# A four-layer graph network on one core: bounds of row numbers kept in registers, and norms without small operations for mean, variance and epsilon

## What is computed

```python
def _layernorm(x, axis=-1, eps=1e-05):
    m = jnp.mean(x, axis=axis, keepdims=True)
    v = jnp.var(x, axis=axis, keepdims=True)
    return (x - m) / jnp.sqrt(v + eps)
...
h = jnp.maximum(_layernorm(x, axis=-1), 0.0)
x = x + _L0_gnn_ref(h, src, dst)                    # degree-normalised sum of neighbours
h = jnp.maximum(_layernorm(x, axis=-1), 0.0)
x = x + _L1_gnn_ref(h, edge_index, L1_gnn_theta)    # polynomial of the Laplacian, 4 steps
h = jnp.maximum(_layernorm(x, axis=-1), 0.0)
x = x + _L2_gnn_ref(h, ..., src, dst, edge_type_86) # relation weights, gate, self loop
h = jnp.maximum(_layernorm(x, axis=-1), 0.0)
x = x + _L3_gnn_ref(h, src, dst)                    # 10 steps, h = 0.9 * A h + 0.1 * h0
```

## Time and profile before

| what | before |
|---|---|
| runs | 2785.8, 2788.61 and 2793.77 us, median 2788.61 |
| profiled execution | 2789.32 us, span 2779.9 us |
| DVE busy | 1768.5 us, 64% |
| POOL busy | 1800.6 us, 65% |
| PE busy | 430.6 us, 15% |
| ACT busy | 335.7 us, 12% |
| HBM traffic | 77.00 MB, 28 GB/s on average |
| clock granted to PE | 1.0 |

### The profile page before, as it was taken

The page is one execution under the profiler, slowest core; times in us unless marked ns, Lnnn a source line. Parts: engine busy times, 40 slices in busy tenths (PEclk is TensorE's granted clock), DMA queues, the critical chain, the costliest instruction groups (busy, mean ns, idle before and its releaser), DMA issues.

```text
span 2779.9 us, 14498 instructions
## 1 busy us (share of the span) xinstructions
PE 430.6 (15%) x2105; PEld 214.1 (8%) x2105; DVE 1768.5 (64%) x3130; ACT 335.7 (12%) x1043; POOL 1800.6 (65%) x1786
## 2 busy tenths in 40 slices
PE   0000000000010000000000098294195000006000
PEld 0000000000010000000000033031131000006000
DVE  8998896666679967177766678587878921420000
ACT  0000021111100110011111144141042200000000
POOL 6666677777554471575777456766456777466776
DMA  1001022221100130110301100100000120000000
GB/s 20 15 11 26 15 61 50 50 50 31 28 9 6 62 127 22 33 57 20 101 25 18 18 3 4 11 2 6 5 7 8 62 63 10 29 11 7 11 8 8
DMA packets 68026, 77.00 MB, mean 28 GB/s; under 512 B 34799, under 2 KB 60872, under 8 KB 67192
## 3 DMA queue, kind: packets, MB, share of 16 engines
q0 software_dynamic: 56384, 23.45, 6.4%
q1 hardware_dynamic: 5720, 27.38, 2.5%
q10 hardware_dynamic: 5856, 25.60, 2.4%
HBM read 35.67 MB, written 46.87 MB: 30 GB/s over the span
## 4 chain that ended last, share of the span: by engine, by line
DVE 49%; issue 25%; POOL 9%; PE 7%; another core or an unknown queue 6%; DMA 2%; ACT 2%; DVEq 1%; POOLq 0%; ACTq 0%; SPq 0%
POOL out L1568 8%; DVE mf L520 7%; DVE pay L520 4%; DVE z L520 3%; DVE psum L915 3%; DVE outs L520 2%; DVE psum L523 2%; PE psum L2009 2%; DVE mf L902 2%; DVE xs L902 2%; DVE xs L897 2%; PE psum L2010 2%; DVE st L544 1%; DVE mf L897 1%
## 5 line engine op out<-in xcount | busy, mean ns | idle before, releaser
L1562 POOL DMA_INDIRECT xs<-in_x,i_src x196 | 200.0, 1020 | 131.2 <-issue 53.9
L1568 POOL DMA_INDIRECT out<-outs,i_outS x196 | 205.2, 1047 | 117.3 <-issue 60.8
L1562 POOL DMA_INDIRECT xd<-x_rows,i_dstX x196 | 204.6, 1044 | 112.5 <-DVE z L1374 66.7
L1562 POOL DMA_INDIRECT xd<-in_x,i_dst x196 | 205.2, 1047 | 111.2 <-DVE mf L520 42.6
L1562 POOL DMA_INDIRECT mf<-x_rows,i_srcX x196 | 200.5, 1023 | 94.5 <-issue 64.3
L1568 POOL DMA_INDIRECT out<-outs,i_srcX x196 | 196.3, 1001 | 71.5 <-issue 58.9
L1562 POOL DMA_INDIRECT pay<-payload_by_dst,i_rank x196 | 195.1, 996 | 62.6 <-issue 62.6
L520 DVE TENSOR_TENSOR mf<-mf 128x128 f32<-128x128 f32 (+5 forms) x578 | 175.1, 341 | 12.2 <-DVE mf L520 1.9
L520 DVE TENSOR_TENSOR pay<-psum,pay 128x512 f32<-128x512 f32 x196 | 132.5, 688 | 66.5 <-ACT pay L1887 56.2
L2009 PE MATMUL psum<-pay 64*128 64x512 f16 x196 | 117.4, 599 | 117.2 <-ACT pay L1872 77.3
L1932 PE MATMUL psum<-ident,small 128*128 128x128 f32 x4 | 1.6, 501 | 851.2 <-DVE small L960 851.2
(11 more groups left out here) (458 smaller groups left out, 2479.9 us busy)
## 6 DMA issues: line engine op xcount, KB each, us to landing
z<-in_x ACTq DMA_DIRECT2D x14, 624.0 KB
out<-z ACTq DMA_DIRECT2D x14, 624.0 KB
l_first_rows<-mf SPq DMA_DIRECT2D x2, 3234.0 KB, 9.7
outs<-in_x ACTq DMA_DIRECT2D x6, 624.0 KB
out<-outs ACTq DMA_DIRECT2D x6, 624.0 KB
l_own_rows<-pay SPq DMA_DIRECT2D x1, 3626.0 KB, 11.0
payload_by_dst<-z SPq DMA_DIRECT2D x1, 3234.0 KB
x_rows<-z SPq DMA_DIRECT2D x1, 3234.0 KB
```

The lines of the kernel that those rows point to most:

```text
L1562: G.indirect_dma_start(out=dest(k), out_offset=None, in_=table, in_offset=bass.IndirectOffsetOnAxis(ap=idx[:, k:k + 1], axis=0), bounds_ch ...
L1568: G.indirect_dma_start(out=table, out_offset=bass.IndirectOffsetOnAxis(ap=idx[:, k:k + 1], axis=0), in_=source(k), in_offset=None, bounds_ ...
```

## The change

POOL loads the five bounds (`N - 1`, `P * EC - 1`, and three of compact tables) into registers once, at the start of its program, and every `gather` and `scatter` is given a register. The norms keep the sum in place of the mean, and subtract it times 1/32 in one scalar_tensor_tensor (`total` and `dense_m` lie in PSUM); the reduction of the squares goes to `sq_in` itself; and ACT takes the root of sum / 32 + epsilon, with scale and a bias from the new tile `eps`. In the third dense norm ALPHA goes into that scale and a second epsilon, EPS / ALPHA ** 2. What is computed stays the same up to rounding. The rest of the diff replaces bounds by `last[...]` in each call.

```diff
--- before.py
+++ after.py
@@ -533,23 +534,30 @@
                     chain(V.reciprocal(o, c["sq_out"][:, 0:w]))
                 return root
 
-            root_main = roots("root_in", "root_out")
-            norms, feeds = [0], [0]
+            root_count, norms, feeds = [0], [0], [0]
+
+            def root(o, a):
+                root_count[0] += 1
+                V.tensor_copy(c["sq_in"][:, 0:EC], a).then_inc(s["root_in"], 1)
+                dve.wait_ge(s["root_out"], root_count[0])
+                link(V.reciprocal(o, c["sq_out"][:, 0:EC]))
 
             def layernorm(xin, hout, tmp, w=EC):
 
-                m, v = c["st1"][:, 0:w], c["st2"][:, 0:w]
-                mean, scale = MEAN[:, 0:w], SCALE[:, 0:w]
+                squares = c["sq_in"]
+                total, scale = MEAN[:, 0:w], SCALE[:, 0:w]
                 sides = (slice(0, w // 2), slice(w // 2, w))
-                link(V.tensor_reduce(m, xin, AX.X, ALU.add))
-                link(ts(mean, m, 1.0 / D, None, ALU.mult))
+                link(V.tensor_reduce(total, xin, AX.X, ALU.add))
                 for side in sides:
-                    tt(tmp[:, side, :], xin[:, side, :], bc(mean[:, side]), ALU.subtract).then_inc(s["norm_centred"], 1)
-                for k, side in enumerate(sides):
-                    dve.wait_ge(s["norm_squared"], 2 * norms[0] + k + 1)
-                    link(V.tensor_reduce(v[:, side], hout[:, side, :], AX.X, ALU.add))
-                link(ts(v, v, 1.0 / D, EPS, ALU.mult, ALU.add))
-                root_main(link, scale, v, w)
+                    V.scalar_tensor_tensor(out=tmp[:, side, :], in0=bc(total[:, side]), scalar=-1.0 / D, in1=xin[:, side, :],
+                                           op0=ALU.mult, op1=ALU.add).then_inc(s["norm_centred"], 1)
+                root_count[0] += 1
+                dve.wait_ge(s["norm_squared"], 2 * norms[0] + 1)
+                link(V.tensor_reduce(squares[:, sides[0]], hout[:, sides[0], :], AX.X, ALU.add))
+                dve.wait_ge(s["norm_squared"], 2 * norms[0] + 2)
+                V.tensor_reduce(squares[:, sides[1]], hout[:, sides[1], :], AX.X, ALU.add).then_inc(s["root_in"], 1)
+                dve.wait_ge(s["root_out"], root_count[0])
+                link(V.reciprocal(scale, c["sq_out"][:, 0:w]))
                 norms[0] += 1
                 V.scalar_tensor_tensor(out=hout, in0=tmp, scalar=0.0, in1=bc(scale), op0=ALU.max, op1=ALU.mult).then_inc(s["normed"], 1)
...
-                root_main(link, o, a)
-
-
             link(V.memset(xd_t[:], 0.0))
             link(V.memset(xs_t[:], 0.0))
+            link(V.memset(eps[:, 0:1], EPS))
+            link(V.memset(eps[:, 1:2], EPS / ALPHA ** 2))
             for n in ("kp0", "kc0", "kn", "et"):
                 link(V.memset(c[n][:], 0.0))
...
@@ -894,13 +900,12 @@
                 for l in range(3):
                     for b in range(nb):
                         X3 = X[b].rearrange("p (c f) -> p c f", f=D)
-                        chain(V.tensor_reduce(dst1[b][0:pn, 0:cn], X3, AX.X, ALU.add))
-                        chain(ts(dense_m[b][0:pn, 0:cn], dst1[b][0:pn, 0:cn], 1.0 / D, None, ALU.mult))
-                        tt(rows(dxc[b][0:pn, 0:w]), X3, bc(dense_m[b][0:pn, 0:cn]), ALU.subtract).then_inc(s["dense_xc"], 1)
+                        chain(V.tensor_reduce(dense_m[b][0:pn, 0:cn], X3, AX.X, ALU.add))
+                        V.scalar_tensor_tensor(out=rows(dxc[b][0:pn, 0:w]), in0=bc(dense_m[b][0:pn, 0:cn]), scalar=-1.0 / D, in1=X3,
+                                               op0=ALU.mult, op1=ALU.add).then_inc(s["dense_xc"], 1)
                     for b in range(nb):
                         dve.wait_ge(s["dense_sq"], number(l, b))
-                        chain(V.tensor_reduce(dst2[b][0:pn, 0:cn], rows(dsq[b][0:pn, 0:w]), AX.X, ALU.add))
-                        ts(dst2[b][0:pn, 0:cn], dst2[b][0:pn, 0:cn], 1.0 / D, EPS, ALU.mult, ALU.add).then_inc(s["dense_var"], 1)
+                        V.tensor_reduce(dst2[b][0:pn, 0:cn], rows(dsq[b][0:pn, 0:w]), AX.X, ALU.add).then_inc(s["dense_var"], 1)
                     for b in range(nb):
                         X3 = X[b].rearrange("p (c f) -> p c f", f=D)
                         dve.wait_ge(s["dense_root"], number(l, b))
@@ -908,8 +913,6 @@
                         chain(V.reciprocal(scale, dst3[b][0:pn, 0:cn]))
                         if l == 1:
                             chain(ts(scale, scale, theta_sum[0:pn], None, ALU.mult))
-                        if l == 2:
-                            chain(ts(scale, scale, ALPHA, None, ALU.mult))
                         dve.wait_ge(s["dense_xc"], number(l, b))
                         h = dense_h[b][0:pn, 0:w]
...
@@ -1556,6 +1559,8 @@
 
         @block.gpsimd
         def _(pool):
+            last = {n: pool.to_reg(n - 1) for n in (N, P * EC, P * W, P * W2S["l1"], P * W2S["l3"])}
+
             def gather(dest, table, idx, bound, sm, n=EC, first=0):
 
                 for k in range(first, first + n):
@@ -1601,7 +1606,7 @@
             for k in range(EC):
                 if k >= AHEAD:
                     pool.wait_ge(s["dve"], turns[min(k - AHEAD, len(turns) - 1)])
-                gather(lambda k: XD[:, k, :], x, icols["dst"], N - 1, s["xdst_in"], 1, k)
+                gather(lambda k: XD[:, k, :], x, icols["dst"], last[N], s["xdst_in"], 1, k)
             pool.wait_ge(s["srows_idx"], 1)
 
...
@@ -1738,7 +1743,9 @@
                 for k, side in enumerate((slice(0, w // 2), slice(w // 2, w))):
                     act.wait_ge(s["norm_centred"], 2 * norms[0] + k + 1)
                     S.activation(hout[:, side, :], tmp[:, side, :], ACT.Square).then_inc(s["norm_squared"], 1)
-                root(1)
+                roots[0] += 1
+                act.wait_ge(s["root_in"], roots[0])
+                S.activation(c["sq_out"][:, 0:w], c["sq_in"][:, 0:w], ACT.Sqrt, bias=eps[:, 0:1], scale=1.0 / D).then_inc(s["root_out"], 1)
                 norms[0] += 1
 
             def feed(source):
@@ -1772,7 +1779,8 @@
                         S.activation(dsq[b][0:pn, 0:w], dxc[b][0:pn, 0:w], ACT.Square).then_inc(s["dense_sq"], 1)
                     for b in range(nb):
                         act.wait_ge(s["dense_var"], number(l, b))
-                        S.activation(dst3[b][0:pn, 0:cn], dst2[b][0:pn, 0:cn], ACT.Sqrt).then_inc(s["dense_root"], 1)
+                        S.activation(dst3[b][0:pn, 0:cn], dst2[b][0:pn, 0:cn], ACT.Sqrt, bias=eps[0:pn, l // 2:l // 2 + 1],
+                                     scale=1.0 / (D * (ALPHA ** 2 if l == 2 else 1.0))).then_inc(s["dense_root"], 1)
 
```

More of the change, by code:

```diff
@@ L1621, in _ @@
             pool.wait_ge(s["l1_own_stored"], 16 * len(OWN_PARTS))
-            gather(lambda k: OWN1[:, k, :], tables["l1", "own"], owni, P * EC - 1, s["l1_own_in"], W)
+            gather(lambda k: OWN1[:, k, :], tables["l1", "own"], owni, last[P * EC], s["l1_own_in"], W)
             pool.wait_ge(s["l1_first_stored"], 16)
-            gather(lambda k: M1[:, k, :], tables["l1", "first"], pf0, P * EC - 1, s["l1_first_in"], W)
+            gather(lambda k: M1[:, k, :], tables["l1", "first"], pf0, last[P * EC], s["l1_first_in"], W)
             pool.wait_ge(s["fits1_set"], 1)
@@ L1636, in _ @@
                     pool.wait_ge(s["l1_third_stored"], 16 * k + 16)
-                    gather(lambda q: M3[:, q, :], tables["l1", "third"], pf3, P * w2 - 1, s["l1_third_in"], w2)
-                    scatter(x2_dram, lambda q: OWN1[:, q, 0:X2W], homei, P * EC - 1, s["x2c_out"], share, share * k)
+                    gather(lambda q: M3[:, q, :], tables["l1", "third"], pf3, last[P * w2], s["l1_third_in"], w2)
+                    scatter(x2_dram, lambda q: OWN1[:, q, 0:X2W], homei, last[P * EC], s["x2c_out"], share, share * k)
                 pool.wait_ge(s["x2c2_ready"], 1)
-                scatter(x2_dram, lambda q: OWN2[:, q, 0:X2W], home2i, P * EC - 1, s["x2c_out"], w2)
+                scatter(x2_dram, lambda q: OWN2[:, q, 0:X2W], home2i, last[P * EC], s["x2c_out"], w2)
                 pool.wait_ge(s["x2c_out"], 16 * (W + w2))
@@ L1658, in _ @@
                             pool.wait_ge(s["l2_done"], 2 + done)
-                        gather(dest, x2_dram, icols[idx], P * EC - 1, s[f"{landed}{part}"], 1, k)
+                        gather(dest, x2_dram, icols[idx], last[P * EC], s[f"{landed}{part}"], 1, k)
                         ahead += 1
@@ L1671, in _ @@
                         pool.wait_ge(s["l2_done"], 2 + 4 * L2_TURNS[2][0] + beside)
-                    scatter(out, lambda q: OUT[:, q, :], icols["outS"], N - 1, s["outs_scattered"], 1, k)
+                    scatter(out, lambda q: OUT[:, q, :], icols["outS"], last[N], s["outs_scattered"], 1, k)
             pool.wait_ge(s["l3_zero"], 1)
             pool.wait_ge(s["l3_own_stored"], 16)
-            gather(lambda k: OWN1[:, k, :], tables["l3", "own"], owni, P * EC - 1, s["l3_own_in"], W)
```

(15 more changed lines are left out.)

20 lines of the change are left out of this document (10 added, 10 removed).

## The result

| | before | changed |
|---|---|---|
| median of the runs | 2787.2 us (4 runs, 2783.8 to 2793.8) | 2739.8 us (4 runs, 2736.4 to 2741.5) |
| profiled execution | 2789.3 us, span 2779.9 us | 2739.1 us, span 2737.3 us |
| time outside the span | 9.4 us | 1.8 us |

A forecast was written before the change was run, and what follows sets the result against it. Bounds: DVE's work, DVE held by POOL's runs, and waited-for POOL transfers. Dense norms 135, edge norms 11 and registers 15, less 46 given back, make 115 us: 2789.3 to 2674 us, range 2550 to 2770 us.

The forecast's parts named there:

- the likeliest case: Whole kernel: the forecast of 115 us gained, to 2674 us, given a 45% chance.
- What holds DVE: Dense halves beside POOL's transfer runs: DVE gets through one instruction per 1.39 us, whatever its length; a half takes 73 us.
- Dense norms: Ten dense halves, each cut from 52 to 38 instructions: 72, 42, 11 and 7 us; 135 us with the tail.
- the tail: Short last chunk of the dense norms: loses 7 operations, half of them held, worth 3 us.
- my lower bound: Dense halves: each removed instruction worth only its own price everywhere, 10 x 3.3 = 33 us.
- Edge norms: Sixteen norms over the edges lose three operations each, worth 11 us.
- Bounds in registers: POOL's transfers: no bound load before each, 0.04 us on 382 waited-for transfers, 15 us; ends 0 and 115.
- What comes back: List-making and first relation tiles: faster DVE meets POOL's runs there and gives back 46 us, ends 0 and 92.
- All of it comes back: Rival, 10%: POOL's runs set both ends of the overlaps; only 54 us remain, about 2735 us.
- Own length: Rival, 20%: in dense halves each operation is worth its own length, held halves 70 us; 60 us gained, 2729 us.
- Hold gone: Rival, 12%: register loads in POOL's stream hold DVE; without them dense halves all take 49 us; 197 us gained, 2592 us.
- Slower: Rival, 9%: closer POOL transfers crowd DVE out, 2.1 us per held instruction; 48 us lost, 2837 us.

The follow-up runs named there:

- the added writes: Changed kernel with 14 writes of a constant put back into each dense half: median 2756.9 us, ratio 0.9874; two halves take 148.5 us.
- the spaced run: Kernel before with a POOL write ahead of each of 196 payload transfers, which then start 1.71 us apart: 2834.4 us, ratio 1.0131.
- two experiments: Changed kernel with bounds as numbers again: 2783.8 us, ratio 0.9933; kernel before with only the dense norms' change: 2788.6 us, ratio 0.9958.
- the run without rows ahead: Changed kernel with POOL sending no source rows ahead of the list-making (ROWS_AT_ONCE 0 instead of 60): 2727.0 us, ratio 0.9734.

## Why the prediction was wrong

The direction and the range held; the size didn't, and the likeliest case was the wrong one. By its own steps:

- **What holds DVE: right in part.** Held stretches exist and cost 1.40 us an instruction whatever its length (the added writes show it), and POOL has a part in them (the spaced run). But POOL's run at 1.30 us is neither enough (late halves free at 46.4 us, 73 list instructions in 30 us) nor needed once DVE is held (12 transfers in 40 us). And I took them for a property of the kernel; they are also one of the conditions under which it runs.
- **Dense norms, 132 us beside 3 for the tail: right and somewhat small.** Measured: 282.8 - 205.2 = 78 us for the first four (I said 72), 198.3 - 139.1 = 59 for the late (42), 60.5 - 46.4 = 14 for the middle one (11). The late ones fall to 46.4 us and not 53, since they are no longer held at all; why 38 instructions escape the hold there, and not in the first halves (52.7 us), no run shows. For the tail, 7 operations with half of them held are 5 us by my own prices, not 3. Where nothing is held, a half of 52 instructions takes 49.4 us and one of 38 takes 46.4, 3.0 us for 14 or 0.21 us each: this is the instruction's own length, near my lower bound. The Trainium skill's fixed cost (VectorE: DVE Perf Modes, in the section on the TRN2 errata) gives an estimated 0.2 us for such an operation, and the trace agrees. In held stretches an instruction takes 1.40 us, some seven times that estimate.
- **Edge norms, 11 us:** 5 to 7 us between two experiments, near the noise.
- **Bounds in registers, 15 us: wrong step, near size.** The gap between transfers is 0.30 us with the loads and without them, so this term is 0. The Trainium skill's 50 ns, cited there (DMA: Bandwidth & Descriptors), are for the dispatch of a DMA and not of a register load. The registers gave 24 us elsewhere: 7.8 outside the span, behind its last instruction, which the sum had no term for, and some 16 in it, whose cause is open.
- **What comes back, 46 us (ends 0 and 92): the step that failed.** The traces show 91 us lost between the end of the first halves and `spread`, where I had 36, and 65 us at the first tiles, where I had 10. I let the hold end soon after POOL's 60 free rows: 32 list instructions for 24 us, and 12 us for the paced transfers. But POOL goes on with two transfers for five held instructions, and the hold lasts with that, even with POOL waiting 3 us at a time: of the 102 nearly all were held. In the first tiles I counted DVE's price alone; PE and ACT are held too, and a tile that each passes to the next costs 20 to 22 us instead of 1.8. That the first loss matters at the end is shown by the run without rows ahead, worth some 24 us; the second was not tested under the hold.
- **The rivals.** "All of it comes back", at 10%, gives 2735 us and names what happened: DVE hardly moves in the overlaps. It is the nearest, in part by luck: 36 of its 54 us come from faster transfers (13 + 8 + 15), of which there are none. "Own length" gives 2729 us by a mechanism that the held halves rule out (53 us, not 70), but is what the dense halves do without a hold. "Hold gone" came for the late halves alone, and by the norms' 38 instructions, not by the registers: with registers alone a late half still takes 72.8 us. "Slower" did not come: the held price stayed at 1.4 us.

## What to carry to other kernels

When an engine is late for no reason in the profile, removing instructions makes that stretch shorter, but ask first which stretch comes next and whether the same cause reaches it: here some 150 us gone from ten places were worth 12 us at the end, and one constant that lets POOL pause before the lists was worth some 24, on another chip than the changed kernel's. Cost a stage that becomes exposed with all of its short instructions, and on every engine that passes work along. And before tuning to such a cause, time the unchanged kernel again at another hour: tuning for the hold (20 columns ahead) cost 28 us when it was absent.

## What the runs showed that I had not expected

- The same kernel takes 2800 us and 2508 us on the same chip within an hour, with a granted clock of 1.0 both times; the change is worth 1.8% in the one case and 0.3% in the other.
- Held, instructions of DVE start 1.40 us apart, and relation tiles 20 to 22 us; unheld, the same lists beside transfers 1.30 us apart take 38 us instead of 136.
- With 0.4 us more between POOL's transfers (1.71 instead of 1.30 us apart) the early halves are not held: 49.5 us a half against 73. Yet DVE is free beside transfers 1.30 us apart in some stretches of the same kernels, and held beside slower ones in others.
- The time outside the span was 9.1 to 10.0 us with bounds as numbers and 1.7 to 1.8 us with registers, in every run under the first conditions, and the difference lies behind the last instruction; under the others it was 1.8 us for both.
